# Second attention of a two-layer kernel: queries computed in rows, squares summed by ScalarE's accumulator, query parts turned by DMA, joined norm weight applied to the keys

## The reference

```python
q = (hidden @ Wq.T)  -> 32 heads of 128;   k, v = ctx @ Wk.T, ctx @ Wv.T -> 8 heads of 128
q = rmsnorm(q, q_norm_w)          # eps 1e-5, over the 128 of a head
k = rmsnorm(repeat(k, 4), k_norm_w)
probs = softmax(q @ k.T / sqrt(128) + mask)     # within one batch of 64 rows
x = x + (probs @ repeat(v, 4)) @ Wo.T           # hidden is layernorm(x)
```

## Time and profile before

| | |
|---|---|
| median of 3 runs | 1529.99 us (1526.86 to 1531.73) |
| span of the profiled execution | 1530.6 us |
| PE busy | 1490.5 us (97%) |
| DVE busy | 1152.5 us (75%) |
| ACT busy | 819.6 us (54%) |
| POOL busy | 710.4 us (46%) |

### The profile page before, as it was taken

How to read it: one execution, slowest core, us unless ns; L and a number is a source line. 1 busy time by engine, 2 the same in 40 slices (tenths; PEclk the granted TensorE clock), 3 DMA queues, 4 the chain that set the end, 5 groups by cost and what they waited for, 6 DMA issues and landing times.

```text
span 1530.6 us, 28713 instructions
## 1 busy us (share of the span) xinstructions
PE 1490.5 (97%) x10919; PEld 874.2 (57%) x10919; DVE 1152.5 (75%) x2139; ACT 819.6 (54%) x2497; POOL 710.4 (46%) x670
## 2 busy tenths in 40 slices
PE   6999999999999899999999999999999999999998
PEld 4888645555554555556555555555565556555554
DVE  4888777778877878677777777786687677678868
ACT  5678731212222775465556655664665565556853
POOL 5668875554564453342333233333433343334553
PEclk9999999999999999999999999999999999999999
DMA  7454345442434252322221221212112112111322
GB/s 245 148 170 137 122 85 118 105 72 42 75 76 76 74 135 46 94 53 33 57 62 31 53 68 24 62 38 55 53 46 56 49 42 56 29 29 35 53 46 111
DMA packets 223642, 113.25 MB, mean 74 GB/s; under 512 B 207264, under 2 KB 207392, under 8 KB 220816
## 3 DMA queue, kind: packets, MB, share of 16 engines
q1 hardware_dynamic: 222208, 104.07, 28.0%
q10 hardware_dynamic: 1296, 7.34, 1.5%
HBM read 57.89 MB, written 4.19 MB: 41 GB/s over the span
## 4 chain that ended last, share of the span: by engine, by line
PE 57%; DVE 4%; ACT 2%; POOL 2%; DMA 1%; issue 1%; SPq 0%; DVEq 0%
PE bank L75 18%; PE bank L77 17%; PE bank L76 17%; PE bank L2451 3%; ACT a_prob L1814 1%; PE bank L2425 1%; DMA a_pT_lo<-a_p_lo 1%; POOL a_prob L1680 1%; PE bank L2426 1%; DVE x_res L2188 1%; POOL a_p_hi L1686 0%; DVE x_res L2032 0%; POOL a_prob L1688 0%; DVE a_nmx L2077 0%; DVE w L2026 0%
## 5 line engine op out<-in xcount | busy, mean ns | idle before, releaser
L1814 ACT ACTIVATE a_prob<-a_prob,a_nmx 128x64 f32<-128x64 f32 x512 | 170.2, 333 | 236.7 <-DVE a_nmx L2077 236.7
L75 PE MATMUL bank<-w,a_oT_hi 128*128 128x512 f16 x512 | 194.0, 379 | 1.5 <-DVE a_oT_lo L2101 1.4
L77 PE MATMUL bank<-w,a_oT_hi 128*128 128x512 f16 x512 | 194.0, 379 | 0.0
L76 PE MATMUL bank<-w,a_oT_lo 128*128 128x512 f16 x512 | 194.0, 379 | 0.0
L2032 DVE SCALAR_TENSOR_TENSOR x_res<-bank,a_oinv,x_res 128x512 f32<-128x512 f32 x128 | 95.8, 748 | 121.5 <-PE bank L77 121.4
L1680 POOL TENSOR_TENSOR a_prob<-a_prob,a_mask 128x512 f32<-128x512 f32 x64 | 79.9, 1270 | 209.7 <-DVE a_prob L2071 209.7
L1159 ACT CAST f_h_hi<-h 128x448 f16<-128x448 f32 x64 | 35.6, 563 | 209.6 <-DVE h L1233 209.6
L1692 POOL TENSOR_TENSOR a_krs<-a_kve,neg_half 128x4 f32<-128x4 f32 x32 | 32.5, 1014 | 244.0 <-DVE a_kve L2056 244.0
L1686 POOL TENSOR_TENSOR a_p_hi<-a_prob,a_rden 128x512 f16<-128x512 f32 x64 | 67.9, 1060 | 111.0 <-DVE a_rden L2085 111.0
L1097 POOL TENSOR_TENSOR f_h_lo<-h,f_h_hi 128x448 f16<-128x448 f32 x64 | 72.7, 1140 | 91.4 <-ACT f_h_hi L1159 91.4
L1695 POOL TENSOR_TENSOR a_qrs<-a_qve,neg_half 128x8 f32<-128x8 f32 x64 | 103.9, 1642 | 12.9 <-DVE a_qve L2046 12.9
(11 more groups left out here) (362 smaller groups left out, 4541.0 us busy)
## 6 DMA issues: line engine op xcount, KB each, us to landing
shared<-in_l_wq SPq DMA_DIRECT2D x8, 1024.0 KB, 5.1
shared<-in_l_wo SPq DMA_DIRECT2D x8, 1024.0 KB, 5.3
shared<-in_w ACTq DMA_DIRECT2D x8, 896.0 KB, 4.7
craw<-in_w SPq DMA_DIRECT2D x11, 512.0 KB, 3.8
a_wide<-in_l_ctxT SPq DMA_DIRECT2D x16, 256.0 KB, 3.9
x_res<-in_x SPq DMA_DIRECT2D x16, 256.0 KB, 4.4
shared<-in_ctx SPq DMA_DIRECT2D x16, 256.0 KB, 4.2
shared<-in_l_wkv SPq DMA_DIRECT2D x8, 512.0 KB, 3.9
```

Source lines behind the costliest of these rows:

```text
L75: pe.matmul(out, a_hi, b_hi, start=first, stop=False)
L76: pe.matmul(out, a_lo, b_hi, start=False, stop=False)
L77: return pe.matmul(out, a_hi, b_lo, start=False, stop=last)
L1814: ins = act.activation(pt, pt, ACT.Exp, bias=nmx[:, col:col + 1], accum_out=den[:, col:col + 1])
```

## The change

It does the following, in the second attention only:

- PE's `query` swaps its operands: rows stationary, weights moving; the bank is now 128 rows x 512 (four heads of 128), one bank per tile t of rows. The count and shape of these matmuls stay.
- ACT's `query` writes qr_hi (plain scale), and then squares each head's 128 columns with the accumulator: four more instructions per bank. `query_squares` and `squares_hi` go, on all engines, and with them the 32 small matmuls a step.
- DVE's `query` makes qr_lo after the squares; `squares_lo` goes; `query_sums` is four instructions that also move the sums to where the scores need them.
- SP's new `queries_T` turns qr_hi and qr_lo by four DMA transposes of 64 partitions x 2048 columns each, issued between `probs_T` (and `rows_T`) and `keys_T`. The scores wait for them.
- The joined norm weight is now a row of 128, kept on all partitions, and multiplies the keys: DVE writes kn (float32) from PSUM, ACT makes kn_hi from it, and DVE makes kn_lo from kn and kn_hi in a new `keys_lo`.
- At the end of the first layer's feed-forward, the weight vectors come in broadcast, and two small DVE instructions (one more than before) join them and take the largest.

```diff
+        qr_hi, qr_lo = sb("qr_hi", [P, TPC, G * HD], F16), sb("qr_lo", [P, TPC, G * HD], F16)
+        qT_hi, qT_lo = sb("qT_hi", [P, 2, TPC * G, S], F16), sb("qT_lo", [P, 2, TPC * G, S], F16)
+        qss = sb("qss", [P, 2, TPC, 2])
+        squares = oT_lo[:, :, :].bitcast(BF16)
@@ sync
+            def queries_T(n):
+                if n:
+                    sp.wait_ge(s_s, n * 2)
+                for to, rows, s_ok, value in ((qT_hi, qr_hi, s_qact, hi_done(n, TPC - 1)), (qT_lo, qr_lo, s_ql, lo_done(n, TPC - 1))):
+                    sp.wait_ge(s_ok, value)
+                    for b in range(2):
+                        sp.dma_start_transpose(to[:, b, :, :], rows[b * S:(b + 1) * S, :, :].rearrange("p t f -> p (t f)"))\
+                          .then_inc(s_qT, 16)
             keys_T(0)
+            queries_T(0)
...
                     if g * NCH + c < last:
+                        queries_T(g * NCH + c + 1)
                         keys_T(g * NCH + c + 1)
@@ scalar
+            def query(n, t):
+                act.wait_ge(s_q, n * TPC + t + 1)
+                if n and t == 0:
+                    act.wait_ge(s_qT, 64 * n)
+                    act.wait_ge(s_qve, n)
+                act.activation(qr_hi[:, t, :], q_banks[t][:, :], ACT.Copy, scale=SUM_DOWN).then_inc(s_qact, 1)
+                for h in range(G):
+                    ins = act.activation(squares[:, t * G + h, :], q_banks[t][:, h * HD:(h + 1) * HD], ACT.Square, scale=SUM_DOWN,
+                                         accum_out=qss[:, h % 2, t, h // 2:h // 2 + 1])
+                ins.then_inc(s_qact, 1)
+            def keys(n):
+                for h in range(2):
+                    rows = slice(2 * h, 2 * h + 2)
+                    act.wait_ge(s_kn, n * 2 + h + 1)
+                    act.copy(kn_hi[:, h * 2 * P:(h + 1) * 2 * P], kn[:, rows, :].rearrange("p t f -> p (t f)")).then_inc(s_knh, 1)
@@ scalar, body
                 if first_step:
-                    act.wait_ge(s_s, 2)
-                    for j in range(2):
-                        query(1, j)
-                        query_squares(1, j)
+                    query(1, 0)
+                    query(1, 1)
                 exps(i, 0)
                 exps(i, 1)
@@ vector
+            def query(n, t):
+                dve.wait_ge(s_qact, squares_done(n, t))
+                dve.scalar_tensor_tensor(qr_lo[:, t, :], q_banks[t][:, :], SUM_DOWN, qr_hi[:, t, :], ALU.mult,
+                                         ALU.subtract).then_inc(s_ql, 1)
             def query_sums(n):
-                dve.wait_ge(s_qss, n + 1)
-                dve.tensor_scalar(qve[:, :], sum_bank[:, 0:TPC * G], qeps[:, :], qgain[:, :], ALU.add, ALU.mult)\
-                   .then_inc(s_qve, 1)
+                dve.wait_ge(s_qact, squares_done(n, TPC - 1))
+                if n:
+                    dve.wait_ge(s_qrs, n * 2)
+                for b in range(2):
+                    for h in range(2):
+                        rows = slice(b * S, (b + 1) * S)
+                        ins = dve.tensor_scalar(by_scores(qve[h * S:(h + 1) * S, :], b), qss[rows, h, :, :], qeps[rows, :],
+                                                qgain[rows, :], ALU.add, ALU.mult)
+                ins.then_inc(s_qve, 1)
             def keys(n, banks=kv_banks):
+                dve.wait_ge(s_krs, n + 1)
                 for t in range(TPC):
-                    if t % 2 == 0:
-                        dve.wait_ge(s_knh, n * 2 + t // 2 + 1)
-                    rows = bass.ts(t, P)
-                    ins = dve.scalar_tensor_tensor(kn_lo[:, rows], banks[t // 2][:, (t % 2) * 2 * HD:(t % 2) * 2 * HD + HD],
-                                                   krs[:, t:t + 1], kn_hi[:, rows], ALU.mult, ALU.subtract)
+                    ins = dve.scalar_tensor_tensor(kn[:, t, :], banks[t // 2][:, (t % 2) * 2 * HD:(t % 2) * 2 * HD + HD],
+                                                   krs[:, t:t + 1], wqk[:, :], ALU.mult, ALU.mult)
+            def keys_lo(n):
+                for h in range(2):
+                    rows = slice(h * 2 * P, (h + 1) * 2 * P)
+                    dve.wait_ge(s_knh, n * 2 + h + 1)
+                    dve.tensor_tensor(kn_lo[:, rows], kn[:, 2 * h:2 * h + 2, :].rearrange("p t f -> p (t f)"), kn_hi[:, rows],
+                                      ALU.subtract).then_inc(s_knl, 1)
@@ vector, body
                 keys(i + 1)
+                keys_lo(i + 1)
                 add_out(c, i, 0)
@@ tensor
+                rows = slice(t * P, (t + 1) * P)
                 for k in range(KD):
-                    ins = split_mm(pe, q_banks[j][:, :], wq_hi[:, k, cols], wq_lo[:, k, cols],
-                                   xT_hi[c][:, k, :], xT_lo[c][:, k, :], k == 0, k == KD - 1)
+                    ins = split_mm(pe, q_banks[t][:, :], xT_hi[c][:, k, rows], xT_lo[c][:, k, rows],
+                                   wq_hi[:, k, :], wq_lo[:, k, :], k == 0, k == KD - 1)
             def scores(i, u):
                 if u == 0:
                     pe.wait_ge(s_kT, 32 * (i + 1))
-                    pe.wait_ge(s_ql, after_dve(i, "lo3"))
+                    pe.wait_ge(s_qT, 64 * (i + 1))
             def attend(i, u, e):
                 pe.wait_ge(s_pT[u], 32 * (i + 1))
-                if u == 0 and i < last:
-                    pe.wait_ge(s_ql, after_dve(i + 1, "sq_lo1"))
             def out_rows(i, t, weights=None, banks=o_banks):
-                if t == 1 and i < last:
-                    pe.wait_ge(s_qve, i + 2)
+                if t < 2 and i < last:
+                    pe.wait_ge(s_ql, lo_done(i + 1, 2 + t))
@@ tensor, body
                 attend(i, 1, c % 2)
-                query_squares(i + 1)
                 out_rows(i, 0, o_weights)
```

More of the change, by code:

```diff
@@ L1569, in stage_l1_attention_gated_ffn @@
         q_banks = [bank[2], bank[3], bank[0], bank[1]]
[L1570 to L1575, removed]
+        hi_done = lambda n, t: (n * TPC + t) * 2 + 1
+        squares_done = lambda n, t: (n * TPC + t) * 2 + 2
+        lo_done = lambda n, t: n * (TPC + 1) + t + (0 if n else 1)
+        out_hi_done = lambda i: (i + 1) * (TPC + 1) + TPC
         kv_banks = [bank[2], bank[3]]
@@ L1580, in stage_l1_attention_gated_ffn @@
         blocks = lambda ap: ap.rearrange("p (b s) -> p b s", s=S)
[L1581 removed]
+        by_scores = lambda ap, b: ap.rearrange("p (t r b) -> p t r b", t=TPC, r=2)[:, :, :, b]
         def run(eng, body):
@@ L1800, in keys_values @@
                 ins.then_inc(s_kvact, 1)
-            def keys(n, banks=kv_banks):
-                act.wait_ge(s_krs, n + 1)
-                for t in range(TPC):
-                    ins = act.activation(kn_hi[:, bass.ts(t, P)], banks[t // 2][:, (t % 2) * 2 * HD:(t % 2) * 2 * HD + HD],
-                                         ACT.Copy, scale=krs[:, t:t + 1])
-                    if t % 2:
-                        ins.then_inc(s_knh, 1)
+            def keys(n):
[3 more added lines that the diff above has]
+                    act.copy(kn_hi[:, h * 2 * P:(h + 1) * 2 * P], kn[:, rows, :].rearrange("p t f -> p (t f)")).then_inc(s_knh, 1)
             def exps(i, u):
@@ L2360, in _ @@
             spread_ctx(2)
+            dve.wait_ge(s_gain, 3)
             keys(0, first_kv)
             query(0, 0)
+            keys_lo(0)
             split_o(0)
@@ L2417, in keys_values @@
                         ins.then_inc(s_kv, 1)
-            def query_squares(n):
-                pe.wait_ge(s_ql, after_dve(n, "sq_lo3"))
-                pe.wait_ge(sum_by_ok, 2)
-                for t in range(TPC):
-                    for b in range(G):
-                        out, at = sum_bank[:, t * G + b:t * G + b + 1], (slice(None), b // 2, 2 * t + b % 2, slice(None))
-                        pe.matmul(out, q2_hi[at], sum_by[:, 0:1], start=True, stop=False)
-                        ins = pe.matmul(out, q2_lo[at], sum_by[:, 1:2], start=False, stop=True)
-                ins.then_inc(s_qss, 1)
             def scores(i, u):
```

128 lines of the change are left out of this document (33 added, 95 removed).

## The result

The kernel after the change takes 1565.9 us (1565.4 to 1566.4), against 1529.0 for the kernel before on the same chip: a ratio of 1.024, 95% interval 1.023 to 1.0254. It is slower by 37 us; my forecast was 1525.5, so it missed by 40. The profiled execution has a span of 1564.6 us, 34.0 above that of before.

A forecast was written before the change was run, and what follows sets the result against it. TensorE was taken to bound the kernel, busy in all of an undisturbed step. From 1530.0 us, 17 came off for 28 regular steps and 12.6 was added for the first steps: 1525.6, given as 1525.5, range 1514 to 1545.

The forecast's parts named there:

- regular steps: Second attention from step 3 on: each step gains 0.81 - 0.2 = 0.6 us, 28 of them 17 us.
- first steps: Steps 0 to 2 of the second attention: query transposes that nothing hides cost 12.6 us together, ends +6 and +19.
- What goes from TensorE: Second attention: the 32 small sum matmuls of a step go, 0.81 us; queries, scores and the gap change nothing.
- Bank 2 and the low probabilities: Regular steps: key/value tile 0 keeps 0.3 us slack on bank 2, `attend(i, 0)` gets its low probabilities in time; no cost.
- Bank 0, `out_rows(i, 2)`: Regular steps: add_out 0 moves by +0.4 us, so TensorE waits 0.1 to 0.3, taken as 0.2, ends 0 and 0.6.
- The 0.3 more in fourth steps: Fourth step of a group: three more small instructions ahead of add_out 0 make TensorE wait 0.3 us more.
- The transposes' price: SP's queue: each new query transpose takes about 1.4 us and lands after about 3.2; hidden in regular steps.
- (a): Rival: steps 0 to 2 cost little, +6 us instead of +12.6, stalls of 0.1 a step; 1516 to 1520 us, chance 0.21.
- (b): Rival: POOL's power excludes keys_lo subtractions, TensorE waits 1.4 to 1.7 us for bank 0 each step; 1562 us, chance 0.06.
- (c): Rival: 64-partition transposes need about 2 us each, 1532 us, chance 0.11; with 2.8 and more 1560 and above, 0.05.
- (d): Rival: the 0.81 us is filled by a wait for oT_lo or a low part at `out_rows(i, 0)`; 1542 us, chance 0.09.

The follow-up runs named there:

- e1: The changed kernel with VectorE's four query sums moved from ahead of the second outputs to behind add_out 0: 1549.3 us, ratio 1.0138.
- e2: e1 with add_out 1 put ahead of the splitting of query weights in third steps of a group: 1540.4 us, ratio 1.0077.
- e3: The changed kernel with the keys part undone (kn_hi and kn_lo from the bank, joined norm weight left out), sums still in front: 1536.6 us, ratio 1.0055.
- e8: e6 with row statistics and power ahead of POOL's low parts, second norm behind the exponentials, other orders changed: 1519.9 us, ratio 0.9948.
- e4: The changed kernel with only the high query parts transposed, scores reading them for the low ones too: 1552.6 us, ratio 1.0161.
- e5: e2 with the first two steps' row transposes moved one step's place earlier in SP's queue: 1522.7 us, ratio 0.9963.
- e6: e5 with the first queries made and turned earlier, their first transposes in two halves: 1523.6 us, ratio 0.9972.
- e7: The kernel before the change, with its row transposes moved earlier as in e5: 1535.4 us, ratio 1.0051.

## Why the prediction was wrong, point by point

The span grew by 34.0 where I had it shrink by 4.5. This miss of 38.5 us has three parts. The regular steps didn't give the 17 us that I took off. They cost 9.9 instead, most of it in third steps. The first steps cost 25.1 where I had 12.6. That makes 17 + 9.9 + 12.5 = 39.4, and the first layer gave 1.0 back.

**What goes from TensorE** was nearly right: I took 0.81 us a step. With VectorE out of the way (e1, e2, e3, e8) steps last 29.17 to 29.18, 0.73 less than 29.90. The rest is the gap that I had put at nothing: 0.30 us from the last matmul of `attend` to the first of `out_rows`, where it was 0.21 to the first of the sums.

**Bank 2 and the low probabilities** (first and second time of the four): right, no wait in undisturbed steps.

**Bank 0, `out_rows(i, 2)`**: the step that failed for the regular steps. Its mechanism and its place were right; the sum was too small, for two reasons. The term of the query sums was mis-sized: I took 0.13 us for each of three more, against the 0.29 of the one in the earlier trace rows. They take 0.30 each, 1.21 for four, so +0.92 where I had +0.4. An instruction of 8 columns costs as much here as one of 16: the row that I had was the price, and I discounted it without a reason. And I added up wrongly: -0.5 - 0.1 + 0.4 + 0.6 + 0.2 makes +0.6, not +0.4. By my own terms TensorE would have waited about 0.5 and gained 0.3 a step, 9 us and not 17. Measured were 0.66 earlier at the sums and 0.33 less of waiting for ScalarE behind them (I had 0.6 for both), 0.92 for the sums and 0.86 for keys_lo with its hand-overs (I had 0.8): +0.79. TensorE waits 0.73 instead of 0.1 to 0.3 (from the matmul at 971.60 to the one at 972.55 it is 0.95, where 0.22 is the pace), above my upper end of 0.6. Of the 28 steps, only the last gained its 0.73 (30.57 instead of 31.30). The 0.3 more in fourth steps was right (0.27).

**Third steps**: missed altogether. I looked at add_out 0 in a plain step and not at add_out 1 in the step where a 2.35 us splitting stands in front of it. The splitting starts 1.26 us later in the step (25.83 instead of 24.57), behind ACT's high part, which now follows kn_hi and so DVE's keys, and add_out 1 with it, at 28.10 instead of 26.84. That is +1.17 in most of the six steps, 6.4 in all. E2 takes it out. Undoing the keys' part alone (e3) takes 1.64 off a third step, moving the sums alone (e1) 0.40.

**The transposes' price**: mis-sized, and in the queue inside my bounds. I took 1.35 to 1.4 us of queue each and a landing of 3.2; measured were 7.3 to 7.4 for four, 1.8 each on average, and 4.5 and 4.6 to land. That they are hidden in regular steps was right (e4: same 29.90).

**First steps**: the other step that failed. My +7.8 (ahead of the first scores), +3.2, +5.0 and -3.4 (steps 0, 1 and 2) were +10.8, +5.0, +9.2 and +0.1. Ahead of the first scores, the last transpose was issued 1.4 us later than I had it, counted from the first query, and landed 4.7 later instead of 3.2. Step 1 by my own terms: rows begin 16.3 after the scores (I had 15.7), take 11.8 (10.5), four queries 7.3 (5.4), keys and landing 4.7 (3.8): 40.1 instead of 35.4. Each term was low, all in one direction. I had taken the row transposes at 10.5 although eight at my own 1.35 make 10.8. In step 2 the late DVE did go, as I said, but the lower clock behind the long wait ahead of it (0.54 over the first 4.7 us) and 2.1 us of waits for add_out and oT_lo took its place. I had put the clock at 0.6 in step 1, and in step 2 inside the 0.7 by which my 30.6 lies above an undisturbed step.

**The rivals.** (a), first steps that cost little: refuted, they cost twice my 12.6. (b), VectorE's subtractions locked out by POOL's power: refuted. In the trace after they run from 970.80 to 971.74 while the power runs from 968.58 to 971.82, and take 0.94 for both; in e1 they take 0.94 too, and there the power starts only behind them (963.18 and 965.98). A delay at add_out 0 did decide, but it came from elsewhere: 0.79 took the whole gain, 0.06 (e1) took nothing; the 0.6 that I named between them isn't tested. (c), 2 us each: true for three transposes in four. How much of the first steps' excess is theirs isn't separated from the clock and the late start of the rows; half of the transposes are worth 13 us (e4). (d), the 0.81 filled by another wait: that is what happened in effect, at `out_rows(i, 2)` and not at `out_rows(i, 0)`, which TensorE reached at 18.8, 0.72 earlier than before, with no wait. With (c) and (d) both, my own figures give 1542 + 6 = 1548; what lacks to 1566 is the third and fourth steps, steps 3 and 4, and the other terms of the first steps. I had treated the cases as exclusive, and the range had no place for two at once.

## What to carry to other kernels

An edit that takes work from the bound engine moves every deadline of the others forward by the same time, so the slack to compare is the old slack less the gain, in every kind of step and not only in the plain one. Price a small instruction as a whole one: the row of its neighbour, whatever its number of columns. Add up the terms of such a sum twice: 0.2 us too little in each of 28 steps is 6 us of forecast. Where a change moves work to a DMA queue, add up the queue's occupancy for the few steps that nothing hides; moving other transposes to where the queue is empty brought back 14 us in two steps here (e2 to e5).

## What I had not expected of the hardware

A VectorE copy or tensor_scalar of SBUF to SBUF, of 4 to 128 columns, was held until a train of GpSimd's tensor operations had ended: 4.08 us for a 128x128 copy (0.23 elsewhere) in e6, ended with POOL's fourth subtraction, and 2.65 and 2.79 for a 128x4 tensor_scalar (0.17 where POOL is idle) in e5 and e7. The four bn_stats (BATCH_NORM_STATS2) ahead of it in e5, the last two of them beside the same POOL operations, took the 2.46 us that they take in e6 with POOL idle:

```profile
518.89 2.46 DVE L93 BATCH_NORM_STATS2 ln_st<-x_res 128x6 f32<-128x512 f32 x4
...
521.81 2.65 DVE L103 TENSOR_SCALAR ln_nm<-ln_mv 128x4 f32<-128x4 f32 x1
...
519.96 4.47 POOL L1711 TENSOR_TENSOR a_xr_lo<-xln,a_xr_hi 128x512 f16<-128x512 f32 x4
```

The Trainium skill, SBUF — State Buffer, "SBUF: two separate sides", has GpSimd's operations and VectorE's two-port modes exclude each other for a whole instruction; the copy agrees with that, except that it was held through several POOL instructions. The same section says it of VectorE operations with two SBUF inputs beside any GpSimd operation that reads SBUF; the subtractions beside the 128x8 power (0.94 us for two, as without it in e1) don't agree.

A transpose from 64 partitions of 2048 columns took 4.5 to 4.6 us to land, though it has only twice the elements of a 128x512 one (2.4 to 2.5), for which I have no reason. And the time that a transpose holds SP's queue goes by the one ahead of it: behind a 128x512 one a large transpose holds it for 1.26 us, behind another large one for about 2.0.
